# Two relu networks and a category layer in fp32: both half steps of the first step by eight products of blocks, and token parts reordered at the ends of blocks

## What is computed

```
def _dense(x, wi_, wo_):
    return relu(x @ wi_) @ wo_          # 512 -> 2048 -> 512
s0 = _dense(x, swi[0], swo[0]); s1 = _dense(x, swi[1], swo[1])
eo = relu(x @ wi[type]) @ wo[type]      # type: one of 5, by batch
w  = softmax(relu(concat(eo[:,0], s0[:,0], s1[:,0]) @ g1) @ g2)
x  = x + eo*w[0] + s0*w[1] + s1*w[2]
x  = x + (x @ W[cat] + b[cat])          # cat: one of 64, by batch
```

## Time and profile before

| | us |
|---|---|
| median of three runs (lowest, highest) | 1955.7 (1954.87, 1956.18) |
| the profiled execution: its time, its span | 1956.29, 1954.4 |
| PE busy | 1933.9, 8510 matmuls |
| DVE busy | 1343.6 (69%) |
| ACT busy | 981.7 (50%) |
| POOL busy | 402.1 (21%) |

### The profile page before, as it was taken

How to read it: one execution, slowest core, us unless ns; L and a number is a source line. 1 busy time by engine, 2 the same in 40 slices (tenths; PEclk the granted TensorE clock), 3 DMA queues, 4 the chain that set the end, 5 groups by cost and what they waited for, 6 DMA issues and landing times.

```text
span 1954.4 us, 25279 instructions
## 1 busy us (share of the span) xinstructions
PE 1933.9 (99%) x8510; PEld 1597.6 (82%) x8510; DVE 1343.6 (69%) x1508; ACT 981.7 (50%) x1438; POOL 402.1 (21%) x283
## 2 busy tenths in 40 slices
PE   7999999999999999999999999999999999999999
PEld 6888888887888888888888888888878888888887
DVE  8888888898576556565655545589975656555566
ACT  5766766756454334444554344456555433344342
POOL 3234224322211111331111111122321111111120
PEclk9999999999999999999999999999999999999999
DMA  6876777768876666786776676578777776656642
GB/s 219 300 292 249 292 279 295 278 242 304 277 256 217 204 204 215 266 293 211 261 258 204 193 224 209 189 278 295 267 279 257 239 228 221 216 182 211 224 156 97
DMA packets 192321, 468.29 MB, mean 240 GB/s; under 512 B 17476, under 2 KB 58436, under 8 KB 185924
## 3 DMA queue, kind: packets, MB, share of 16 engines
q1 hardware_dynamic: 192196, 466.69, 69.8%
HBM read 319.82 MB, written 146.80 MB: 239 GB/s over the span
## 4 chain that ended last, share of the span: by engine, by line
PE 73%; DVE 2%; DMA 1%; issue 1%; ACT 1%; SPq 0%; ACTq 0%; DVEq 0%
PE ups L1555 35%; PE rps L1555 35%; PE aps L1555 3%; DMA XT<-xT_kept 1%; DVE WD L1173 0%; DVE XL L1157 0%; DVE HL L1186 0%; DVE HT L737 0%; ACT XH L843 0%; ACT HH L938 0%; DVE ACC L1205 0%; DVE XT L1512 0%; ACT WD L874 0%; DVE XL L1518 0%; PE aps L1654 0%
## 5 line engine op out<-in xcount | busy, mean ns | idle before, releaser
L1555 PE MATMUL ups<-XH,WU 128*128 128x512 f32 x2660 | 878.0, 391 | 14.1 <-issue 4.4
L1555 PE MATMUL rps<-HH,WD 128*128 128x512 f32 x2672 | 876.5, 389 | 0.6 <-ACT rps L953 0.6
L1555 PEld LDWEIGHTS ups<-XH,WU 128*128 128x128 f32 x2660 | 501.7, 189 | 123.0 <-issue 11.0
L1555 PEld LDWEIGHTS rps<-HH,WD 128*128 128x128 f32 x2672 | 501.3, 188 | 105.4 <-DVE HL L1186 1.3
L1555 PE MATMUL rps<-HL,WD 128*128 128x512 f32 x1336 | 519.7, 389 | 0.0
L1555 PE MATMUL ups<-XL,WU 128*128 128x512 f32 x1330 | 519.3, 390 | 0.0
L737 POOL TENSOR_TENSOR HT<-hid 128x512 f32<-128x512 f32 x96 | 133.2, 1388 | 1316.8 <-PE rps L1555 1298.2
L1186 DVE TENSOR_TENSOR HL<-HT,HH 128x1024 fp32r<-128x1024 f32 x240 | 290.2, 1219 | 9.6 <-ACT HH L938 5.1
L1208 DVE SCALAR_TENSOR_TENSOR ACC<-rps,gw,ACC 128x1024 f32<-128x1024 f32 x126 | 161.6, 1282 | 196.6 <-PE rps L1555 196.3
L1555 PEld LDWEIGHTS rps<-HL,WD 128*128 128x128 f32 x1336 | 251.0, 188 | 52.1
L1555 PEld LDWEIGHTS ups<-XL,WU 128*128 128x128 f32 x1330 | 250.6, 188 | 51.5
(11 more groups left out here) (129 smaller groups left out, 1521.7 us busy)
## 6 DMA issues: line engine op xcount, KB each, us to landing
WU<-wu_kept SPq DMA_DIRECT2D x448, 256.0 KB, 3.5
WD<-wd_kept SPq DMA_DIRECT2D x224, 512.0 KB, 3.3
wd_kept<-WD SPq DMA_DIRECT2D x112, 512.0 KB, 3.5
wu_kept<-WU SPq DMA_DIRECT2D x31, 1024.0 KB, 4.9
wu_kept<-WU SPq DMA_DIRECT2D x31, 768.0 KB, 4.5
sums_kept<-ACC SPq DMA_DIRECT2D x28, 512.0 KB, 5.4
MB<-sums_kept SPq DMA_DIRECT2D x28, 512.0 KB, 5.7
XS<-in_x_dram SPq DMA_DIRECT2D x21, 512.0 KB, 5.8
```

What stands on the lines that cost most here:

```text
L1555: ins = pe.matmul(dst, stationary[a], moving[c], start=start and j == 0, stop=stop and j == 2, skip_group_check=True)
```

## The change

**Start.** Half step 1 is now done by the eight plain products too: `plain(n, p)` for n = 0, 1, with the banks ups and aps for n = 1. PF has room for two halves; the second one is loaded in the place in SP's queue where PUR of half 1 was, and split by `first_up_high(1, k)`, `first_up_low(1, k)` into the second half of the WD slots. `up_sums(1)`, `up_high(1)`, `up_low(1)`, the copies, block_22 and block_21 of half step 1 fall away (which is why all their counts are one less), and `up_sums(3)` moves ahead of the loop. The first half step with seven products is n = 2.

**Block sums.** They are made in step 0 (for half 0) and in step 1 (for half 1): SP loads the raw blocks a second time, into SR, POOL sums them in place, ACT and DVE split them, SP stores them. SR and WS have changed places. The loads and sums of the next block's tokens (`load_ahead(1)`, `ahead_sum`, `keep_ahead`) therefore start a step later.

**Ends of blocks.** In the `start` step ACT splits parts 4 and 5 ahead of HH of part 3 and does the copies w and u earlier; DVE does add_sum of the last down product and part 4 ahead of the hidden sums and part 5 ahead of HL of part 1.

The pieces below are, in order: constants and PF, SP, the banks, POOL, ACT, DVE, and PE's list.

```
-X_ORDER_FIRST = [0, 6, 3, 1, 2, 4, 5]
+X_ORDER_FIRST = [0, 6, 3, 1, 2, 5, 4]
-B12_USED = 3
+B12_USED = PRODUCTS + 3
...
-        PF = sb("PF", [P, 4, HB], F32, at=hh_at + 5 * 4 * KB)
+        PF = sb("PF", [P, 2, 4, HB], F32, at=hh_at + 4 * 4 * KB)
...
+            def first_blocks_again(n):
+                sp.wait_ge(s_xlo, PRODUCTS)
+                if n > 0:
+                    sp.wait_ge(s_wsl, 2 * n)
+                sp.dma_start(SR[:, :, :], swi[0, n, :, :, :]).then_inc(s_sr, 16)
...
+            first_blocks(1)
-            blocks_up(1, None)
             blocks_up(2, None)
+            blocks_up(3, None)
...
+                    if m < 2 and i == 0:
+                        first_blocks_again(m)
...
+        plain_banks = [[rps[0][:, 0, :], rps[0][:, 1, :], rps[1][:, 0, :], rps[1][:, 1, :]],
+                       [ups[1], ups[0], ups[2], aps[:, :]]]
...
+            def first_up_sums(n):
+                k = 4 * n
+                A11, A12, A21, A22 = (SR[:, q, :] for q in range(4))
+                pool.wait_ge(s_sr, 16 * (n + 1))
...
+            def first_sums_high(n, q):
+                act.wait_ge(s_S0, 4 * (n + 1))
+                act.wait_ge(s_xlo, PRODUCTS)
+                if n > 0:
+                    act.wait_ge(s_wsk, 32 * n)
...
                 if start:
                     token_high(s + 1, 4)
-                if d >= 0:
-                    hidden_high(d, 3)
-                if more:
+                    token_high(s + 1, 5)
                     seventh_product(a)
+                hidden_high(d, 3)
+                if more and not start:
+                    seventh_product(a)
+                if start:
+                    chain(a)
                 made(m - 1, PRODUCTS - 1)
...
                 if start:
                     token_low(s + 1, 3)
+                    second(0)
+                    token_low(s + 1, 4)
                 hidden_sum(dve, d, 1, 0)
                 hidden_sum(dve, d, 1, 1)
                 hidden_sum(dve, d, 1, 3)
+                if start:
+                    token_low(s + 1, 5)
...
-            for p in range(len(PLAIN)):
-                plain(p)
-            for i in range(PRODUCTS):
-                up(1, i)
+            for n in range(2):
+                for p in range(len(PLAIN)):
+                    plain(n, p)
```

More of the change, by code:

```diff
@@ L845, in up_high @@
             def up_high(n, late):
-                if n > 1:
+                if n > 2:
                     act.wait_ge(s_up, PRODUCTS * (n - 1) + (PRODUCTS if late else EARLY))
                     act.wait_ge(s_wuk[late], 16 * PREP_HALF[n])
-                act.wait_ge(s_Su, 4 * (PREP_HALF[n] - 1) + (4 if late else 3))
+                act.wait_ge(s_Su, 4 * (PREP_HALF[n] - 2) + (4 if late else 3))
                 if late:
@@ L930, in hidden_high @@
                     if i == 1:
-                        act.wait_ge(s_relu, relus + 3)
+                        act.wait_ge(s_relu, relus + (3 if N > 0 else 4))
                     else:
@@ L1011, in _ @@
             token_high(0, 3)
+            for k in range(4):
+                first_up_high(1, k)
             token_high(0, 1)
             token_high(0, 2)
-            up_high(1, 0)
-            first_relu(4)
-            first_relu(5)
-            up_high(1, 1)
-            first_relu(6)
-            first_relu(7)
-            first_product(1)
+            first_relu(0, 4)
+            first_relu(0, 5)
+            first_relu(0, 6)
+            first_relu(0, 7)
+            up_high(2, 0)
+            up_high(2, 1)
+            token_high(0, 5)
+            first_relu(1, 4)
             token_high(0, 4)
-            seventh_product(1)
-            chain(1)
-            token_high(0, 5)
-            relu_11(1)
+            first_relu(1, 5)
+            first_relu(1, 6)
             hidden_high(0, 0)
-            up_high(2, 0)
-            relu_22(1)
-            relu_21(1)
-            relu_12(1)
-            up_high(2, 1)
+            first_relu(1, 7)
             down_high(0, 0)
@@ L1061, in _ @@
                     token_high(s + 1, 4)
-                if d >= 0:
-                    hidden_high(d, 3)
-                if more:
+                    token_high(s + 1, 5)
                     seventh_product(a)
+                hidden_high(d, 3)
[3 more added lines that the diff above has]
+                    chain(a)
                 made(m - 1, PRODUCTS - 1)
-                if d >= 0:
-                    hidden_high(d, 2)
-                if start:
-                    token_high(s + 1, 5)
+                hidden_high(d, 2)
                 second(0)
-                if more:
+                if more and not start:
                     chain(a)
@@ L1090, in _ @@
                     relu_22(a)
-                if m == 0:
-                    first_sums_high(0)
-                    first_sums_high(1)
+                if m < 2:
+                    first_sums_high(m, 0)
+                    first_sums_high(m, 1)
                 if d >= 0:
@@ L1336, in first_B12_low, with first_sums_low @@
                 dve.tensor_tensor(XL[:, 4, :], XS[:, 1, :], XH[:, 4, :].bitcast(F32), ALU.subtract).then_inc(s_b12l, 1)
-            def first_sums_low(late):
-                part = slice(2 * late, 2 * late + 2)
-                dve.wait_ge(s_wsh, late + 1)
+            def first_sums_low(n, q):
+                part = slice(2 * q, 2 * q + 2)
+                dve.wait_ge(s_wsh, 2 * n + q + 1)
                 dve.tensor_tensor(WS[:, part, 1, :], SR[:, part, :], WS[:, part, 0, :].bitcast(F32),
@@ L1345, in _ @@
             for k in range(4):
[L1346 removed]
+                first_up_low(0, k)
             first_B12_low()
@@ L1349, in _ @@
             token_low(0, 3)
+            for k in range(4):
+                first_up_low(1, k)
             token_sum(dve, 0)
             token_sum(dve, 1)
-            up_sums(1)
             token_low(0, 1)
-            up_low(1, 0)
+            up_sums(2)
             token_low(0, 2)
+            up_low(2, 0)
+            up_low(2, 1)
+            token_sum(dve, 3)
+            token_low(0, 5)
             token_sum(dve, 2)
-            token_sum(dve, 3)
-            up_low(1, 1)
+            up_sums(3)
             token_low(0, 4)
-            token_low(0, 5)
-            up_sums(2)
-            block_22(1)
-            block_21(1)
-            up_low(2, 0)
             hidden_low(0, 0)
-            up_low(2, 1)
             down_low(0, 0)
@@ L1419, in _ @@
                 hidden_low(d, 1)
-                second(0)
-                if start:
-                    token_low(s + 1, 4)
-                    token_low(s + 1, 5)
+                if not start:
+                    second(0)
                 if d >= 0:
@@ L1447, in _ @@
                     hidden_low(d, 5)
-                if m == 0:
-                    first_sums_low(0)
-                    first_sums_low(1)
-                if m in (2, 3, 4):
-                    ahead_sum(dve, 1, m - 2)
+                if m < 2:
+                    first_sums_low(m, 0)
+                    first_sums_low(m, 1)
+                if m in (3, 4, 5):
+                    ahead_sum(dve, 1, m - 3)
                 if m == 6:
```

174 lines of the change are left out of this document (86 added, 88 removed).

## The result

The changed kernel takes **1960.52 us** (median of 10 runs, 1959.83 to 1961.75); the kernel before, run beside it, 1955.12 (10 runs, 1953.90 to 1957.18). The ratio is 1.0027, 95% interval 1.0017 to 1.0037: **slower by 5.4 us**, where the forecast was 2.75 us faster and the range ended at 1956.8. The profiled execution took 1959.83 (span 1958.1), 3.5 above the profiled one of before.

What follows compares the result with a forecast made beforehand. PE was taken as the bound, busy 1933.9 of 1954.4 us, with only idle time and slow matmuls to win. Start 1.4 plus ends 1.4 - 0.75 + 0.7 gave 2.75 off 1955.7: 1953.0 us, range 1949 to 1956.8.

Steps and rivals of the forecast that it cites:

- The bound and the start: PE up to its first down product: one long stop before up(2, 1), down product at 45.1 not 46.61, 1.5 us gained.
- 13.05 us lost at the start: Kernel before, 18.60 to 46.61: PE's 11 products take 28.01 instead of 14.96 us; about 9.6 of the loss are gaps.
- Step 0: SR reload and POOL sums make ACT 0.8 us late, slack takes it: counted 0, 1.4 of 1.5 kept; bounds 0 to 3 lost.
- 4 x 0.5: Step 0: time in us that DVE loses beside POOL's four sums, set against four block sums less on DVE.
- 0.8 at up(3, 2): Step 0: PE's slack in us, from first_product(3) done at 60.74 to PE's arrival at 61.57.
- Rival (c): Step 0, ACT at first_sums_high: late SR reload and POOL sums stop PE, slower, 1960 us; chance 0.08.
- my 53.4: Step 0: time in us at which POOL is done with its sums, after SR lands at 49.8.
- Step 1: The added 1.3 and 2 us of DVE lie before up_low(5, 1), needed 3 us later: 0, bounds 0 to 1.5.
- DVE has idle time behind it: Step 1: in a PE step of 38 us, DVE's idle time takes the added work, cost 0.
- any wait of PE in steps 2 to 6: Sign that would show the forecast wrong: PE waiting anywhere in these steps; no size given.
- The ends: Three block ends: +1.4, -0.75 and +0.7 us, with one PE wait each on DVE's block_22 of 2.5, 0.75 and 2.2.
- The rival with low clock at each end (b): Low clock follows merged gaps, costing 1.65 us at first and third ends: nothing gained, 1956.3 us; chance 0.14.

Runs made afterwards that it cites:

- e2: The kernel before with only the orders of ACT and DVE at the ends of blocks changed to the new ones: 1955.30 us, ratio 1.0001.
- e7: The kernel before with four more DVE operations (2.87 us together) ahead of block_21 in step 1: 1958.00 us, ratio 1.0011.
- e11: The kernel before with the four added DVE operations of e7 put into step 7 instead of step 1: 1958.78 us, ratio 1.0016.
- e1: The changed kernel with the orders of ACT and DVE at the ends of blocks as before: 1961.64 us, ratio 1.0035 to the kernel before.
- e9: The changed kernel with only the SR reload for half step 0 issued earlier, as in e5: 1957.39 us, ratio 1.0007 to the kernel before.
- e10: The changed kernel with only the SR reload for half step 1 moved into step 0, as in e5: 1957.94 us, ratio 1.0008 to the kernel before.
- e5: The changed kernel with both SR reloads issued earlier (first after the third token sum, second in step 0): 1953.19 us, ratio 0.9989 to the kernel before.
- e12: e5 with the old ACT and DVE order at the second block end, the new at first and third: 1953.35 us, ratio 0.9985 to the kernel before.
- e3: The changed kernel with half step 0's block sums made from PF without a reload, half step 1 unchanged: 1957.01 us, ratio 1.0009 to the kernel before.
- e4: The changed kernel without POOL's eight block-sum operations, so the sums are missing from the result: 1953.82 us, ratio 0.9993 to the kernel before.
- e6: The changed kernel with ACT's start reordered: half 1's first three ReLUs before token part 5, part 4 behind first_product(2): 1960.07 us, ratio 1.0024 to the kernel before.

## Why the prediction was wrong

**The bound and the start: right.** The one stop before up(2, 1) was 3.97 (forecast 4.1), the first down product came at 45.40 (45.1), the third token sum ended at 32.58 + 2.28 = 34.9 (34.4). How much of this the median has is less clear. The lag at 49.3 us differs between executions of the same start: 0, -2.35, -0.50 and -0.71 in the four traces with the start of before (the kernel before, e2, e7, e11), mean -0.9; -1.18, -2.84, -0.83, -2.78 and -1.34, -2.50 in the traces of the changed kernel, e1, e9, e10, e5 and e12, mean -1.9. With the -0.61 of e3 and the -3.42 of e4, whose starts have the same order too, the mean stays -1.9. So about 1.0 gained, where I had 1.5, and a spread of over 2 us, which makes the 1.0 a rough number. The profiled execution of before was on the late side, 1.2 over its median, and that of the changed kernel 0.7 under its own. That is why the medians differ by 5.4 and the profiled executions by only 3.5. One reading of mine was off without any use made of it: of the 13.05 us lost at the start 8.7, not 9.6, are idle time.

**Step 0: here it failed, at "I count 0, with 1.4 kept".** Three numbers of that step were off, all the same way. The load: issued at 42.79 (42.3) and 7.9 long (7.5), so 0.9 late. POOL: I had four sums at 0.87, as the first row of the kernel before had it; there the four end at 38.29, 3.3 us after 34.95, in part beside DVE's block_22 and block_21, which read a bank:

```profile
37.49 0.80 POOL L772 TENSOR_TENSOR SR<-PF,SR 128x256 f32<-128x256 f32 x1
```

Beside the three DVE rows shown above they took 0.74, 1.72, 1.19 and 1.60, 5.2 in all, so 1.7 late. I had charged DVE for the meeting ("4 x 0.5") and POOL nothing. And ACT was at first_sums_high at 51.8, not 52.6: in the kernel before it had stood 0.87 us for DVE's block_22 just ahead of it, and DVE, with four block sums less in this step, no longer keeps it waiting. Late by 4.27 instead of 0.8, against a slack of 2.2 (e5) at up(3, 1), which I had not walked through; I had 0.8 at up(3, 2). Rival (c) is this mechanism, engine and queue, and I gave it 0.08, with SR landing after 52.5 as the condition for a loss. SR landed at 50.7; POOL ended 2.6 us after my 53.4, of which 0.9 is the landing and 1.7 POOL's own time. That (c) names 1960 and 1960.5 was measured is luck: its 1960 stood for POOL 6.7 us late in step 0.

**Step 1: failed the same way, and worse.** I let "DVE has idle time behind it" carry it, and did not ask when ACT comes to the sums: it stood 4.37 us there. DVE was busy 34.1 of 38 us in the kernel before, so nearly 4 us were free, but that room was no help once its work slid under POOL's (e7). Direct stops and slower matmuls cost 2.0, the small losses up to 210 us 1.5. I had named "any wait of PE in steps 2 to 6" as a sign against me; it came.

**The ends: nearly right in sum, wrong in the waiting engine.** Forecast +1.4 -0.75 +0.7 = 1.35; measured +1.3 -1.0 +0.6, about 0.9 to 1.0, by the traces of e2 and of the changed kernel. The first size was right, the second and third off by 0.25 and 0.1. At the first and third end it was not block_22 on which PE waited, but ACT's copy of the first down product (L970, at 477.06; at 1441.12 at the third end), held up by HH of part 3, whose sum DVE does later now:

```profile
471.26 1.06 ACT L955 ACTIVATE HH<-HT 128x1024 fp32r<-128x1024 f32 x1 [2.09 <-DVE HT L752]
...
477.06 1.07 ACT L970 ACTIVATE rps<-rps 128x512 f32<-128x512 f32 x2
```

At the second end DVE stood at add_sum as worked out (3.1 forecast):

```profile
951.19 1.28 DVE L1225 SCALAR_TENSOR_TENSOR ACC<-rps,gw,ACC 128x1024 f32<-128x1024 f32 x1 [3.01 <-PE rps L1572]
```

but the product stopped was a down product that waits for HL (0.50, at 959.81 above), with a few slower matmuls behind it.

**The clock.** The rival with low clock at each end (b) did not come: in the changed kernel the granted clock was 1.00 from 470 to 483, from 955 to 962 and from 1434 to 1446 us. That nearly the same gaps are not always followed by the same level, is what the starts show: with the start's code unchanged and stops of 2.21 and 2.22 us in the kernel before, 2.00 and 2.23 in e11, the granted clock from 30 to 36 us was 0.72 in the first and 1.00 in the second. This agrees with what the Trainium skill (TensorE: Matmul & The Clock Gate, "What's actually happening") says, that the chip's look at the activity is not tied to the kernel's start.

## What to carry to other kernels

Price work that is moved beside other work on both engines: POOL's four sums took 5.2 us beside two-input operations of DVE against 3.3 before, and I had stretched only DVE. Look at where a load is issued and at what waits behind it: the same 512 KB took 3.1 us alone and 7.9 us in the queue behind stores and another load, and moving it turned a loss of 5.4 us into a gain of 2.7 (e5); but the late load cost PE nothing once POOL's sums behind it were left out (e4). And "this engine has idle time behind it" need not absorb a delay when its work, once late, meets an engine that slows it: then a single delay can be paid again in later steps, as in e7, until a stretch with real room.

## What was new about the hardware

- A POOL sum of 256 elements a row took 0.74 us beside DVE's block_22, which reads one tile and a PSUM bank, and 1.1 to 1.8 beside DVE operations with two inputs in SBUF (rows of POOL in step 0 and in e5).
- One delay of DVE by 2.9 us cost PE 2.7 us in e7 and 3.5 in e11, about half of it only 35 to 115 us after the delay.
- A stop of PE of 3.06 us was followed by about 6 us at a granted clock of 0.50 (e10), worth 3.1 us; stops of 1.75 (the changed kernel) and 2.69 (e6) at the same place were not, but one of 2.21 elsewhere in e6 was.
- A kernel's starts differ by up to 2.4 us at 49 us between executions of the same code, so effects below 1 us were seen in the lag of a trace and not in medians (e2, e12).
